# Convolution two units ahead and one more turned step in a two-way Mamba layer with a gated feed-forward

## The reference

```python
xz = einsum('bld,ed->ble', x, in_w); u, z = split(xz, 2)
u = silu(conv1d_4taps_per_channel(u) + conv_b)
x_dbl = einsum('bld,ed->ble', u, xproj_w)              # 8 columns of dt, 16 of B, 16 of C
dt = softplus(einsum('blr,dr->bld', x_dbl[..., :8], dt_w) + dt_b)
dA = exp(dt[..., None] * A)                            # A = -exp(A_log), 16 states
dBu = dt[..., None] * Bm[:, :, None, :] * u[..., None]
h = dA_t * h + dBu_t; y = einsum('bdn,bn->bd', h, C_t) # over the 512 tokens
y = (y + u * D) * silu(z)
out = einsum('bld,ed->ble', y, out_w)
# after both directions:
h = silu(x @ w_gate.T) * (x @ w_up.T); out = h @ w_down.T
```

## Time and profile before

| | |
|---|---|
| median of 3 runs | 470.99 us (468.65 to 473.14) |
| the profiled execution | 472.82 us, span 471.0 us |
| DVE busy | 422.3 us, 90% |
| PE busy | 405.1 us, 86% |
| POOL busy | 398.9 us, 85% |
| ACT busy | 374.3 us, 79% |
| first scan starts, last scan ends | 23.1 us, 439.7 us |

### The profile page before, as it was taken

The page is one execution under the profiler, slowest core; times in us unless marked ns, Lnnn a source line. Parts: engine busy times, 40 slices in busy tenths (PEclk is TensorE's granted clock), DMA queues, the critical chain, the costliest instruction groups (busy, mean ns, idle before and its releaser), DMA issues. The chain is left out here.

```text
span 471.0 us, 6668 instructions
## 1 busy us (share of the span) xinstructions
PE 405.1 (86%) x2250; PEld 277.5 (59%) x2250; DVE 422.3 (90%) x338; ACT 374.3 (79%) x732; POOL 398.9 (85%) x239
## 2 busy tenths in 40 slices
...
DMA packets 17777, 43.02 MB, mean 91 GB/s; under 512 B 1616, under 2 KB 7120, under 8 KB 17744
## 3 DMA queue, kind: packets, MB, share of 16 engines
...
...
## 5 line engine op out<-in xcount | busy, mean ns | idle before, releaser
L1123 POOL TENSOR_TENSOR hq<-hq,c_tiles 128x1024 f32<-128x1024 f32 x127 | 298.0, 2366 | 30.6 <-DVE hq L1276 30.3
L1276 DVE TENSOR_TENSOR_SCAN hq<-da,bb 128x1024 f32<-128x1024 f32 x115 | 260.4, 2280 | 9.4 <-PE bb L679 2.9
L909 ACT ACTIVATE da<-dt,neg_a 128x511 f32<-128x511 f32 x230 | 149.8, 711 | 7.4 <-DVE hq L1276 7.2
L707 PE MATMUL ysum<-wts,hq 128*128 128x128 f32 x1024 | 145.9, 290 | 7.7 <-ACT y_t L949 4.9
L707 PEld LDWEIGHTS ysum<-wts,hq 128*128 128x128 f32 x1024 | 121.6, 148 | 32.6 <-issue 19.7
L1257 DVE TENSOR_TENSOR bb<-bb,dtu 128x1024 f32<-128x1024 f32 x79 | 95.8, 1213 | 8.3 <-PE bb L652 7.5
L1020 ACT ACTIVATE g<-dtu_t,bc_t 128x256 f32<-128x256 f32 x144 | 61.0, 498 | 0.0
L679 PE MATMUL bb<-wts,g 128*128 128x128 f32 x288 | 43.2, 300 | 8.0 <-ACT g L1020 5.7
L679 PEld LDWEIGHTS bb<-wts,g 128*128 128x128 f32 x288 | 36.4, 154 | 17.6 <-issue 10.2
L652 PE MATMUL bb<-b_rows,pick 48*128 48x512 bf16 x75 | 29.9, 398 | 10.2 <-DVE hq L1276 10.2
L1276 DVE TENSOR_TENSOR_SCAN hq<-bb,dbu 128x1024 f32<-128x1024 f32 x13 | 29.7, 2281 | 6.7 <-issue 4.3
...
## 6 DMA issues: line engine op xcount, KB each, us to landing
...
```

Source lines behind the costliest of these rows:

```text
L707: mm = nc.tensor.matmul(ysum[:, bank, at], hq[:, i % H_RING, h, block(b)], ident, start=opens, stop=(i % NS == NS - 1), is_transpose=True, ...
L909: ins = nc.scalar.activation(da[:, i % DA_RING, h, 1:SEQ], dt[:, k % 2, h, 1:SEQ], ACT.Exp, scale=neg_a[:, c:c + 1])
L1123: nc.gpsimd.tensor_tensor(hq[:, i % H_RING], hq[:, i % H_RING], c_tiles[:, n % C_RING, i % 2, :].unsqueeze(1).broadcast_to([P, 2, SEQ]), A ...
L1276: nc.vector.tensor_tensor_scan(out=hq[:, i % H_RING].rearrange("p h t -> p (h t)"), data0=decay.rearrange("p h t -> p (h t)"), data1=dbu_t ...
```

## The change

It alters the order and two tables; no arithmetic. From unit 1 on `conv_ahead(slot, k + 2)` makes the convolution of the unit after the next: unit 1 makes that of unit 2 in slots 0 to 3 and that of unit 3 in slots 6 to 9; units 2 to 5 make that of unit k+2 in slots 3 to 6, and units 6 and 7 none. In units 2 to 7 `conv_out` (slot 6), `z` (slot 7), the feed-forward's `ffn_gate` (slots 8 and 9) and `dt` (slot 8, or 9 with a feed-forward) stand in a row, and the `exp` of slots 7 up to the slot of `dt` come behind it. `xproj` moves to slot 0, `bc` and `split` to slot 1, `b_rows` to slot 2, `back` to slots 3 and 4 and `gate` to 4 and 5. Step 3 of units 3, 5 and 7 is turned, and the pooled step 8 becomes step 7.

```diff
-TURNED = ((4, 6, 10, 13), (2, 4, 6, 10, 13)) + 3 * ((3, 6, 10, 12, 15), (0, 5, 10, 13))
-POOLED = ((15,), (15,), (8, 14), (15,)) + 2 * ((8, 14), (8, 15))
+TURNED = ((4, 6, 10, 13), (2, 4, 6, 10, 13)) + 3 * ((3, 6, 10, 12, 15), (0, 3, 5, 10, 13))
+POOLED = ((15,), (15,), (7, 14), (15,)) + 2 * ((7, 14), (7, 15))
...
+    def conv_ahead(slot, n):
+        put(slot, *taps(n, 0)[:2])
+        put(slot + 1, *taps(n, 0)[2:])
+        put(slot + 2, *taps(n, 1)[:2])
+        put(slot + 3, *taps(n, 1)[2:], ("conv_out", n, 0), ("conv_out", n, 1))
...
-        g_slot = {2: 0, 3: 0, 4: 1, 5: 1, 6: 2, 10: 6, 12: 9, 13: 8 if ffn else 10, 15: 11}
+        g_slot = {2: 0, 3: 0, 4: 1, 5: 2, 6: 2, 10: 6 if k < 2 else 5, 12: 9, 13: 10, 15: 11}
...
+        if k <= 1:
+            conv, z_slot, back, xproj, bc = (at + 2 - 2 * k, at + 6 - 2 * k, at + 5, at + 7 - 2 * k, at + 8 - k)
+            conv_ahead(conv, n)
+        else:
+            z_slot, back, xproj, bc = at + 7, at + 3, at, at + 1
+        dt_slot = at + (9 if k == 0 else 10 if k == 1 else 9 if ffn else 8)
+        put(z_slot, ("z", k, 0), ("z", k, 1))
...
+        else:
+            for s in range(at + 7, dt_slot + 1):
+                late[s] = dt_slot
+        if k >= 1:
+            put(back, ("back", k - 1, 0))
+            put(back + 1, ("gate", k - 1, 0), ("back", k - 1, 1))
+            put(back + 2, ("gate", k - 1, 1))
+        if k >= 1 and k + 2 < UNITS:
+            conv_ahead(at + (6 if k == 1 else 3), k + 2)
         if more:
-            put(at + lag, *taps(n, 0)[:2])
-            put(at + lag + 1, *taps(n, 0)[2:])
-            put(at + lag + 2, *taps(n, 1)[:2])
-            put(at + lag + 3, *taps(n, 1)[2:], ("conv_out", n, 0), ("conv_out", n, 1))
-        put(at + lag + 4, ("z", k, 0), ("z", k, 1))
-        late[at + lag + 4] = at + lag + 4
...
+            put(xproj, ("xproj_mm", n, 0), ("xproj_mm", n, 1), ("xproj", n))
+            put(bc, ("bc", n), ("split", n))
...
+            sooner[at + 7].append(("turn_x1", q - 1, 0))
+            put(at + 8, ("ffn_gate", q - 1, 0, 0), ("ffn_gate", q - 1, 0, 1))
+            put(at + 9, ("ffn_gate", q - 1, 0, 2))
...
+            put(dt_slot, ("dt_mm", n, 0), ("dt_mm", n, 1), ("dt", n, 0), ("dt", n, 1), ("dtu", n))
+            put(at + (2 if k >= 2 else 11), ("b_rows", n))
```

More of the change, by code:

```diff
@@ L153, in plan @@
         for p in POOLED[k]:
-            put(at + {8: 4, 14: 10, 15: 11}[p], ("mul_b_pooled", at + p))
+            put(at + {7: 3, 14: 10, 15: 11}[p], ("mul_b_pooled", at + p))
         if k == 0:
@@ L162, in plan @@
             put(at + 11, ("down_centre",))
-        if more:
-            put(at + lag, *taps(n, 0)[:2])
-            put(at + lag + 1, *taps(n, 0)[2:])
-            put(at + lag + 2, *taps(n, 1)[:2])
-            put(at + lag + 3, *taps(n, 1)[2:], ("conv_out", n, 0), ("conv_out", n, 1))
-        put(at + lag + 4, ("z", k, 0), ("z", k, 1))
-        late[at + lag + 4] = at + lag + 4
[L172 to L181, removed]
+        if k <= 1:
[5 more added lines that the diff above has]
+        put(z_slot, ("z", k, 0), ("z", k, 1))
+        if k <= 1:
+            late[z_slot] = z_slot
+            if k == 1:
+                late[dt_slot] = dt_slot
+        else:
[7 more added lines that the diff above has]
+            conv_ahead(at + (6 if k == 1 else 3), k + 2)
+        if more:
+            put(xproj, ("xproj_mm", n, 0), ("xproj_mm", n, 1), ("xproj", n))
+            put(bc, ("bc", n), ("split", n))
         if d == 0 and q >= 1:
@@ L188, in plan @@
             put(at + 15, ("ln_var", 2, q - 1, 0), ("ln_pow", 2, q - 1, 0))
[L189 to L192, removed]
+            put(at + 17, ("ln_act", 2, q - 1, 0), ("add_attn", q - 1, 0))
         if ffn:
+            put(at + 3, ("ln_square", 3, q - 1))
+            put(at + 4, ("ln_var", 3, q - 1, 0), ("ln_pow", 3, q - 1, 0), ("ln_shift", 3, q - 1, 0))
+            put(at + 6, ("ln_act", 3, q - 1, 0))
             soon = 0 if more else -2
-            put(at + soon + 7 + 2 * (not more), ("turn_x1", q - 1, 0))
-            put(at + soon + 10, ("ffn_gate", q - 1, 0, 0), ("ffn_gate", q - 1, 0, 1))
-            put(at + soon + 11, ("ffn_gate", q - 1, 0, 2))
-            late[at + soon + 10] = late[at + soon + 11] = at + soon + 11
+            sooner[at + 7].append(("turn_x1", q - 1, 0))
+            put(at + 8, ("ffn_gate", q - 1, 0, 0), ("ffn_gate", q - 1, 0, 1))
+            put(at + 9, ("ffn_gate", q - 1, 0, 2))
             for c in range(3):
```

14 lines of the change are left out of this document (7 added, 7 removed).

## The result

The changed kernel takes **498.1 us** (mean of 495.28, 496.72 and 502.43) where the kernel before took 471.0 in the same comparison (468.65 to 473.14): ratio 1.058, 95% interval 1.046 to 1.070, some 27 us more. The profiled execution took 496.72 us with a span of 494.9. Forecast were 479 us and at most 492: the sign was right, the size far off.

A forecast was written before the change was run, and what follows sets the result against it. VectorE was taken to set the pace, three engines within some 10% of it; unit times from its busy time, turned-step savings and stalls summed to +6.6 on the profiled 472.8, so 479 us, range 462 to 492.

The forecast's parts named there:

- The value taken between throughput and walk: Stalls in units 2 to 5: 8.5 us odd (5.3 to 12), 3.0 us even (1.3 to 3.9).
- The full walk: Following TensorE's queue and waits through a unit: stalls of some 12 us in an odd unit, 3.9 in an even one.
- Step 4: Unit 5: its `bcast` is late because `b_rows` waits for `split`; stall 1.5 to 3 us.
- Step 5: Unit 5: back, taps and fold (4.1 us) stand before its `g_turn`; 1.0 us more stall.
- Step 6: Unit 5: fold, back and taps (4.1 us) stand before its `bcast`; 2.3 us more stall.
- Steps 8 to 11: Unit 5, slots 7 to 10: `turn_x1` waiting for LN 3 costs 2.0 us, the chain ffn_gate, dt 1.8.
- Step 13: Unit 5: its `g` stands behind dt, a load and three `exp`, then turn and `ffn_up`; stall 1.5 to 2.4 us.
- The clock as a rival of its own: Thin slots 1 and 2 halve TensorE's clock for slots 3 and 4: some +4 us each, 491 us, 12%.
- The turned step: Units 3, 5 and 7: one product of 1.29 us leaves VectorE, -3.9 us, all on the path.
- The even units: Units 2 and 4: stalls of 3.0 us (1.3 to 3.9), changing the units by +0.4 and +1.3.
- Units 0 and 1: Unit 0, taps a slot earlier: +0.5 us (0 to +1.5); unit 1, a second convolution: +2.5 (+1 to +4).
- Rival 1: Whole kernel: ScalarE's relief decides and TensorE absorbs its burst in units 2 to 7; 458 us, 22%.

The follow-up runs named there:

- keep_busy_13_fit: Changed kernel with three matmuls that nobody reads ahead of the wait for `g` at step 13 of units 3 and 5: 496.60 us, ratio 1.054.
- mended_two: Changed kernel with `b_rows` moved to slot 11 and the `g` of step 13 in slot 8 of feed-forward units: 484.84 us, ratio 1.029.
- b_rows_late: Changed kernel with `b_rows` moved from slot 2 back to slot 11: 493.27 us, ratio 1.049.
- g13_early: Changed kernel with the `g` of step 13 back in slot 8 of the feed-forward units: 490.23 us, ratio 1.041.
- turned_only: Kernel before with step 3 of units 3, 5 and 7 turned and nothing else: 476.30 us, ratio 1.011.
- hybrid: Kernel before with the changed kernel's order in units 0 and 7: 466.39 us, ratio 0.992.
- hybrid_last: Kernel before with the changed kernel's order in unit 7 alone: 469.29 us, ratio 0.994.

## Why the prediction was wrong

What held:
- VectorE is stalled by TensorE at steps 4, 5, 6, 8, 9, 11 and 13 of unit 5, those that I named, with `b_rows` waiting for `split`. ScalarE's busy time fell from 374.3 to 369.8 us (5 expected).
- Units 6 and 7 together gained 4.9 us (forecast 5.3). By themselves unit 7 gained 6.5 and unit 6 lost 1.6, but how the time falls to the two varies: keep_busy_13_fit has the same order there and 46.5 and 53.7 us, where the changed kernel has 49.4 and 50.4.
- The Trainium skill (ScalarE: Activation LUTs, What ACT_TABLE_LOAD costs) has a drain of about 1.38 us with each table load. It again has no row: after the 1.28 us load at 340.17 the first `dt` starts at 341.46.
- The Trainium skill (TensorE: Matmul & The Clock Gate, Part 1) has the clock of an idle TensorE gated to half rate. The fall at 311.7 us, behind the wait of 2.96, agrees. The one at 342.4 doesn't: TensorE had been busy since 330.6.

What failed. The profiled executions are 23.9 us apart and 6.6 was forecast. The 17.3 us between are units 2 to 5 with 5.8, 4.7, 3.0 and 6.5 us, units 1 and 6 with 1.9 and 2.3, less 5.0 in unit 0 and 1.9 in unit 7.
- **The value taken between throughput and walk.** This is the step that failed. I had walked unit 5 to some 12 us of stalls and took 8.5 for the odd units and 3.0 for even ones, "since a delay at one place eases the next". Nothing eased: unit 5 stalled 14.6 us, unit 3 12.4, units 2 and 4 8.6 and 5.7. mended_two and b_rows_late show it: the gains of the two placements add (4.1 + 8.0, and 13.4 together), and with the delays of steps 4 and 5 gone the one of step 6 stayed, 5.58 us from scan to scan for 5.89. The full walk would have given 479 + 3.5 + 3.5 + 0.9 + 0.9 = 488 us.
- **The walk's own terms.** Step 4: 1.08 us (1.5 to 3). Step 5: 2.51 (1.0). Step 6: 1.87 (2.3). Steps 8 to 11: 4.2 (3.8). Step 13: 4.13 (1.5 to 2.4). At steps 5 and 13 I had TensorE at full clock; the taps took 3.08 for 1.88 and the `g_turn` and `ffn_up` 3.8 for 2.1. At 13 I also counted one table load and there are two (340.17 and 342.57), 1.28 us more. g13_early shows what it came to: 8.0 us, of which the profiled executions have 4.3 and 3.7 at step 13 of units 3 and 5. (The walk's terms add up to 10.1 to 12.5; "some 12" is the upper part of it.)
- **The clock as a rival of its own.** It was no alternative to the forecast but came on top of the waits. By the estimate above it is some 9 us in the profiled execution, not the 4 for each of four units that I gave. The sign that I had set for it, a granted clock under 0.9 in units 2 to 5, didn't come: they have 0.90 to 0.97. It isn't tied to the waits alone either (the fall at 342.4).
- **The turned step, -3.9 us "all on the path".** turned_only has +5: the step's `exp` and its `g_turn` come too late. A product taken off VectorE is worth its 1.29 us only if `g` and `exp` are ready. With this term at 0 the forecast would have been 483 us.
- **The even units.** Their 3.0 us (3.9 at most) left out the `g_turn` of step 6, which stands behind a `back` that waits for `gate` and two taps: VectorE waits 1.6 us there in units 2 and 4 each (in unit 4 the `g_turn` ends at 268.76 and the scan starts at 268.85). And both had matmuls at half clock from scan 4 to 5, 3.6 and 1.5 us by the estimate above. Without these two terms they stalled 3.4 and 2.6 us, close to the walk.
- **Units 0 and 1.** Unit 0 gained 4.5 us where I had +0.5, and unit 1 lost 4.4 where I had 2.5, at most 4. Together they are unchanged (103.6 us for 103.7, forecast +3.0). hybrid kept unit 0's gain, but hybrid_last, with the order before there, has 51.8 us against 54.0 in the profile before, so about half of it comes and goes between executions of one order.

Rival 1, that ScalarE's relief decides, failed: the loads of the changed kernel are worth 6.2 us at most, and TensorE didn't absorb its burst. (Its "best units before" are named the wrong way round, 1.2 us is unit 1 and 1.7 are units 4 and 6; its sum stays the same.)
